# The state's increment in a gated linear attention block: two full-width matmuls, or four of 64 columns in the left and right half of the array

## What is computed

```python
def step(s, inp):
    qi, ki, vi, gi = inp
    s = jnp.exp(gi)[:, :, None, None] * s + ki[..., :, None] * vi[..., None, :]
    o = jnp.einsum('bhk,bhkv->bhv', qi, s)
    return (s, o)
```

## Time and profile before

| | us |
|---|---|
| median of the runs | 3608.03 |
| the profiled execution's own time | 3603.81 |
| its span | 3602.1 |
| TensorE matmuls busy | 3510.2 |
| VectorE busy | 2582.3 |
| ScalarE busy | 1739.2 |
| GpSimd busy | 1180.6 |

### The profile page before, as it was taken

How to read it: one execution, slowest core, us unless ns; L and a number is a source line. 1 busy time by engine, 2 the same in 40 slices (tenths; PEclk the granted TensorE clock), 3 DMA queues, 4 the chain that set the end, 5 groups by cost and what they waited for, 6 DMA issues and landing times. The chain is left out here.

```text
span 3602.1 us, 78492 instructions
## 1 busy us (share of the span) xinstructions
PE 3510.2 (97%) x25989; PEld 3321.8 (92%) x25989; DVE 2582.3 (72%) x5463; ACT 1739.2 (48%) x4352; POOL 1180.6 (33%) x1491
## 2 busy tenths in 40 slices
PE   7999999999999999999999998799999999999998
PEld 7999999999999999999999997689998999899987
DVE  4777777777777777777777777576767676766666
ACT  4556556556556556556555564333333333333332
POOL 0444444444444444444444444211211111111110
PEclk9999999999999999999999998799999999999999
DMA  4332332332332332332332332521122112211220
GB/s 154 96 81 71 104 81 71 104 81 72 101 85 72 96 90 70 93 94 70 92 94 71 91 90 58 190 90 70 73 79 93 70 71 80 93 70 70 82 93 24
DMA packets 243936, 309.04 MB, mean 86 GB/s; under 512 B 22160, under 2 KB 188064, under 8 KB 239792
## 3 DMA queue, kind: packets, MB, share of 16 engines
q1 hardware_dynamic: 243888, 308.42, 28.2%
HBM read 223.40 MB, written 84.93 MB: 86 GB/s over the span
## 5 line engine op out<-in xcount | busy, mean ns | idle before, releaser
L723 DVE TENSOR_TENSOR q_lo<-q,q_hi 64x256 fp32r<-64x256 f32 x512 | 494.0, 965 | 11.4
L849 POOL TENSOR_TENSOR v_lo<-v,v_hi 128x256 fp32r<-128x256 f32 x256 | 188.6, 737 | 734.5 <-ACT v_hi L624 734.5
L637 ACT ACTIVATE prob<-cum_rows,w_cur 128x128 f32<-128x128 f32 x1024 | 328.0, 392 | 132.3 <-POOL cum_rows L839 131.7
L854 POOL TENSOR_TENSOR prob_lo<-prob,prob_hi 128x512 fp32r<-128x512 f32 x256 | 348.8, 1363 | 64.5 <-ACT prob_hi L651 64.4
L55 PE MATMUL psJ<-h_hi,w_g_hi 128*128 128x256 f32 x1024 | 308.0, 301 | 18.1 <-DVE h_lo L707 18.1
L55 PE MATMUL psJ<-h_hi,w_q_hi 128*128 128x256 f32 x1024 | 304.3, 297 | 0.0
L1210 POOL TENSOR_TENSOR rstd<-var_eps,c_minus_half 128x2 f32<-128x2 f32 x64 | 44.6, 697 | 789.8 <-DVE var_eps L1112 434.7
L55 PE MATMUL psG<-h_hi,w_og_hi 128*128 128x256 f32 x1024 | 288.5, 282 | 7.4 <-DMA h_lo<-h_dram 7.4
L57 PE MATMUL psG<-h_hi,w_og_lo 128*128 128x256 f32 x1024 | 288.3, 282 | 0.0
L56 PE MATMUL psG<-h_lo,w_og_hi 128*128 128x256 f32 x1024 | 288.3, 282 | 0.0
L56 PE MATMUL psJ<-h_lo,w_q_hi 128*128 128x256 f32 x1024 | 285.7, 279 | 0.0
(11 more groups left out here) (232 smaller groups left out, 11863.7 us busy)
## 6 DMA issues: line engine op xcount, KB each, us to landing
cum_rows<-cum_dram SPq DMA_DIRECT2D x256, 256.0 KB, 5.3
grown<-cum_dram SPq DMA_DIRECT2D x512, 64.0 KB, 3.3
o_dram<-o SPq DMA_DIRECT2D x256, 128.0 KB, 1.9
o_cols<-o_dram SPq DMA_DIRECT2D x32, 1024.0 KB, 5.9
an_norm_x<-in_L_attn_x_dram SPq DMA_DIRECT2D x32, 512.0 KB, 4.1
h_dram<-h_hi SPq DMA_DIRECT2D x32, 512.0 KB, 4.0
h_dram<-h_lo SPq DMA_DIRECT2D x32, 512.0 KB, 5.2
h_hi<-h_dram SPq DMA_DIRECT2D x32, 512.0 KB, 3.8
```

Source lines behind the costliest of these rows:

```text
L637: last = nc.scalar.activation(prob[:, 2 * c + h, :], cum_rows[:, p % 4, 2 * c + h, :], ACT.Exp, bias=w_cur[:, 0, c, 2 * p + h:2 * p + h + ...
L723: last = nc.vector.tensor_tensor(q_lo[r, :, h, :], q[r, p, :].rearrange("p (c t) -> p c t", c=NC), q_hi[r, :, h, :].bitcast(F32), ALU.subt ...
L849: nc.gpsimd.tensor_tensor(v_lo[:, :, :], v[:, :, p * P:(p + 1) * P], v_hi[:, :, :].bitcast(F32), ALU.subtract).then_inc(s["v_lo"], 1)
L854: nc.gpsimd.tensor_tensor(prob_lo[:, :, :], prob[:, :, :], prob_hi[:, :, :].bitcast(F32), ALU.subtract).then_inc(s["prob_lo"], 1)
```

## The change

Each chunk's increment is formed by two matmuls in place of one. For head h they take the 64 columns of kw and the 64 columns of v that belong to it and write the diagonal block, psK[r, 2 + c, r]; the contraction is over all 128 tokens as before. `tile_position=(0, h * DH)` puts the weights of head 0 in columns 0 to 63 of the array and those of head 1 in columns 64 to 127. The blocks off the diagonal are no longer written. In the built program each of the new matmuls has a tile size of 128 rows by 64 columns, and all the others around it one of 128 by 128.

```diff
@@ -508,8 +508,11 @@
                     pe.wait_ge(s["kw"], n + 1)
                     pe.wait_ge(s["by_act"], act_done(j, ("v", 5 if p > 3 else 3)))
                     for c in range(NC):
-                        last = nc.tensor.matmul(psK[:, 2 + c, :], kw[:, c, :], v[:, c, p * P:(p + 1) * P],
-                                                start=True, stop=True)
+                        for h in range(2):
+                            r = slice(h * DH, (h + 1) * DH)
+                            last = nc.tensor.matmul(psK[r, 2 + c, r], kw[:, c, r],
+                                                    v[:, c, p * P + h * DH:p * P + (h + 1) * DH],
+                                                    start=True, stop=True, tile_position=(0, h * DH))
                     last.then_inc(s["inc"], 1)
```

## The result

The changed kernel takes 3631.1 us (median of four runs, 3630.74 to 3632.53), the one before 3607.8: a ratio of 1.0067, 95% interval 1.0054 to 1.0079. It is 23 us slower (27 us between the two profiled executions, since that of before lay 4 us under its median). The forecast was 3655; direction and range held, the size was double.

The account below looks back on a forecast made before the run. TensorE's stream was taken to bound the first pass. Only the array switches added time, +46.6 us on the profiled 3603.8, giving 3650.4, or 3654.6 as the median; range 3564 to 3692.

Parts of the forecast that it names:

- the prediction's own signs: Around line 513: forecast wrong if both edge distances are the plain 0.11 us or the eight records take clearly under 0.44.
- What bounds the kernel: First pass: it lasts as long as TensorE's stream, busy 2119.6 of 2150 us, with small waits.
- Size alone, 0: Increment: eight records of half size cost the 0.44 us of the four now; 0, bounds 0 to +10 us.
- The switch, 0.09 us: Into and out of the divided array each pair step: 0.09 us each, 0.18 a step, +46.6 us, uncovered loads left out.
- the transposes with 16 rows: Program start: first 16-row transpose comes 0.20 us after the last full one, 0.09 more than a plain successor.
- the stated upper bound of 0.345: Per pair step: two switches of 0.09 us plus uncovered loads of 0.055 going in and 0.11 coming out; 88 us.
- Side by side, 0: Increment: the two heads' matmuls in different array columns run one after another; 0, bounds 0 and -42 us.
- the five of the text: Increment, if halves overlap: five steps of 55 ns in place of eight, 165 ns less a pair step.
- The other engines, 0: Outside TensorE: increment and VectorE's mid ready 0.18 us later, covered by 24 projection matmuls; 0.
- The sum: Whole run: size 0, switches +46.6, side by side 0, other engines 0, giving +46.6 us.
- switch and overlap: Rival for the increment: switches cost 0.18 us, overlap saves 0.165; 3612, up to 3654 with uncovered loads; chance 0.17.

Follow-up runs that it names:

- e10_before_early: The kernel before with ScalarE's exponentials of pair 5 put ahead of the last copy of v, the array not divided: 3597.0 us, ratio 0.9974.
- e4_left: The changed kernel with head 0 computed twice and head 1 left out (but in tile 0), all eight records in the left half: 3684.3 us, ratio 1.0218.
- e5_moving64: The kernel before with each increment's moving operand cut into two of 64 columns, 128 weight columns kept, array never divided: 3714.0 us, ratio 1.0295.
- e2_half: The changed kernel without head 1's increment (but in tile 0), four records a step in the left half: 3630.6 us, ratio 1.0072.
- e3_heads: The changed kernel with both chunks of head 0 first, then both of head 1: 3632.8 us, ratio 1.0075.
- e6_state_first: The changed kernel with the state's full-width matmul (line 518) ahead of the increment and not behind it: 3615.2 us, ratio 1.0023.

## Why the prediction was right or wrong

The direction and the range held, but the mechanism only in part, and the nearness of the forecast is luck. By the prediction's own signs it was wrong: the eight records take 0.38 us with the gap behind them, clearly less than 0.44, and they start in pairs.

- *What bounds the kernel*: right. TensorE is busy for 97 to 98% of the span in all of these kernels, and the 26.5 us that it takes longer for the first pass came out as 27 us of span. One part was too trusting: the waits by matmul left out some 7 to 10 us that an earlier kw brings back (e10_before_early). The changed kernel hides part of its loss there, since TensorE comes later to a kw that was late.
- *Size alone, 0*: right. Eight records one after another cost about what four of full width do: 0.058 us each in e4_left, 0.47 against 0.44, 6 us over the run and within the stated 0 to 10. The load is the floor at 128 columns (e5_moving64).
- *The switch, 0.09 us*: the gap was read rightly from the transposes with 16 rows. It is 0.206 for 0.115 us from matmul to matmul on the way in, and the gap is 0.09 us each way. What failed is the choice to leave the uncovered loads out ("may hold part of a load already"). They come on top, 0.05 going in and 0.10 coming out, and a visit costs 0.34 us, about the stated upper bound of 0.345, not 0.18. Line 538, which shows no gap, was rightly set aside. The Trainium skill's rule of the drain at a change of mode ("TensorEngine Tiling (Array Packing)", key properties) held, and this case puts a price on it.
- *Side by side, 0*: wrong, and this is the step that made the result half of the forecast. The sum took the serial reading because the trace before had no two matmuls in different columns and the nearest rows (16 rows of the array, one part) were one after another, and argued that loads and streams are issued in one order. e2_half, e4_left and e3_heads show a full overlap: four slots, one better than the five of the text, 0.21 us less than one after another and not 0, and the same in another order.
- *The other engines, 0*: right in effect. TensorE's wait for mid fell from 2.5 to 0.8 us. But the increment is not ready 0.18 us later: the way out comes behind it and the overlap ahead of it, and VectorE's wait for it fell from 141.6 us to 111.4.
- *Left out*: the pace of the projections behind the visit, 14 us in the trace, given back by e6_state_first. No term of the sum covered it, and no row named in the prediction pointed to it.
- *The sum*: in an undisturbed step 0.340 for the visit less 0.208 for the overlap makes 0.132 us, 34 us over 256 steps. Averaged over all steps, waits of before included, the step grew by 0.067 us, 17 us: TensorE waits less ahead of the increment, 13 us in the 217 steps behind a projection of g and 4 in the seven of the last tile that no projection precedes. With 14 in q and k that is 31; some 4.5 us less elsewhere, which I haven't placed, make the 26.5 of the table. The rival "switch and overlap" (3612, with uncovered loads up to 3654) named the mechanism; it had the smaller chance, and 3631 lies in the middle of its span, which reaches from below the forecast's own range (3640 to 3692) into its lower part and doesn't just fill that part, as the text has it. The forecast's 3655 came as near as it did by luck, by two errors of opposite sign: 40 us too little for the visits, 53 us of overlap left out.

## What to carry to other kernels

Price a divided array by visits, not by matmuls: each visit between full-width float32 work cost 0.34 us here (two gaps of 0.09 and two loads that nothing covers), each pair of heads done in it gave back 0.21, so one pair in a visit loses and four gain. A price worked out from an idle gap needs the load behind the gap added to it. And when TensorE is the bound, look at the waits of its weight loads as well as those of its matmuls, and at the spacing of untouched lines before and after: here they held 7 to 10 and 14 us.

## What the runs showed of the hardware

- The two column halves work through their own records: 4 records in one half, 8 in two and 32 in two took 4, 4 and 16 slots of 0.058 us; the 8 did so in both orders tried, with the second record of a slot 7 ns behind the first or 13.
- A row of float32r matmuls with 256 moving columns keeps to one of two paces, 113 or 118 ns, as long as nothing makes it wait, and which one goes with what stands ahead of the row: fast behind a divided visit (217 of 217 rows in e6_state_first), slow behind a visit and two float32 records (206 of 217 in the changed kernel), mostly fast behind six float32 records (172 of 217 before) or ten (199 of 217 in e5_moving64). That is not the whole of it: with TensorE's order as before and ScalarE's changed, 190 of 217 are fast (e10_before_early). The granted clock was 1.00 over nearly all of the rows. What sets the pace is open.
